# A z block computed around the last x_proj product, and gate tiles between the turnings at the switch of halves

## The reference, cut to what matters

```
xn = layernorm(x)                                  # x: (2, 1024, 512), everything in float32
xz = xn @ in_proj_w                                # 512 -> 2 * 1024: x and z
xc = silu(causal_conv4(x_part))
dt, B, C = rmsnorm each part of (xc @ x_proj_w.T)  # 32 + 16 + 16 columns
dt = softplus(dt @ dt_proj_w.T + dt_bias)
for each time step t, each of 16 states n, each of 1024 channels:
    h[n] = exp(dt * A[n]) * h[n] + dt * B[n] * xc
    y    = sum over n of C[n] * h[n]
s = ((y + D * xc) * silu(z)) @ out_proj_w.T
g = silu( down( silu(gate(xn)) * up(xn) ) )        # gate, up, down: dequantised weights and a low-rank part
out = x + s * g
```

## Time and profile before

| | |
|---|---|
| median of 3 runs | 1154.04 us (1153.87 to 1154.09) |
| profiled execution | 1153.82 us, of it span 1151.7 us |
| TensorE, VectorE, ScalarE, GpSimd busy | 96%, 80%, 59%, 64% of the span |
| mean granted clock of TensorE | 0.992 |
| chain that ended last | POOL 39%, PE 28%, issue 19%, DVE 11% |

### The profile page before, as it was taken

One profiled execution on the slowest core, in us unless ns is written; L12 is line 12 of the kernel. 1 busy time (PEld: TensorE's weight loads), 2 busy tenths in 40 slices (PEclk: granted clock), 3 DMA queues, 4 the chain that ended last, 5 costly groups with the idle time before them and its releaser, 6 DMA issues.

```text
span 1151.7 us, 12396 instructions
## 1 busy us (share of the span) xinstructions
PE 1103.5 (96%) x4366; PEld 589.5 (51%) x4366; DVE 926.9 (80%) x741; ACT 674.3 (59%) x850; POOL 734.7 (64%) x406
## 2 busy tenths in 40 slices
PE   5998999999999999999999899999999999999998
PEld 3443455555545555554443335555555455555543
DVE  4897999999789999996315469999987899999820
ACT  3224577877647777764022357777775477777410
POOL 2000799999537999980410048999983599999311
PEclk9998999999999999999999899999999999999999
DMA  7663289999914999999411124999984289998941
GB/s 248 218 205 128 100 206 235 249 243 225 247 54 118 241 238 261 209 201 315 174 37 36 46 82 130 239 238 250 240 205 149 84 207 247 242 238 193 280 181 43
DMA packets 62162, 215.44 MB, mean 187 GB/s; under 512 B 6762, under 2 KB 6890, under 8 KB 61588
## 3 DMA queue, kind: packets, MB, share of 16 engines
q0 software_dynamic: 16128, 88.09, 38.8%
q1 hardware_dynamic: 44388, 120.88, 30.9%
q10 hardware_dynamic: 1584, 5.68, 1.2%
HBM read 103.56 MB, written 22.98 MB: 110 GB/s over the span
## 4 chain that ended last, share of the span: by engine, by line
POOL 39%; PE 28%; issue 19%; DVE 11%; ACT 2%; DMA 1%; POOLq 0%; DVEq 0%; SPq 0%
POOL ub L627 34%; PE psM L1076 8%; PE psM L1015 6%; DVE hb L1253 5%; POOL yT L637 5%; PE psA L845 4%; PE psM L876 3%; PE psT L991 2%; DVE xc L1244 1%; DVE th L1103 1%; PE psA L961 1%; DMA yT<-yc 1%; DVE xc L1103 1%; DVE hid L1103 1%; PE psT L840 1%
## 5 line engine op out<-in xcount | busy, mean ns | idle before, releaser
L627 POOL TENSOR_TENSOR ub<-dtx,bn 128x1024 f32<-128x1024 f32 x256 | 647.0, 2590 | 275.0 <-DMA bn<-ss_rows_scratch 187.3
L1253 DVE TENSOR_TENSOR_SCAN hb<-psA,ub 128x1024 f32<-128x1024 f32 x256 | 581.7, 2280 | 26.4 <-POOL ub L627 23.2
L732 ACT ACTIVATE psA<-dt,cc 128x1024 f32<-128x1024 f32 x256 | 285.9, 1119 | 139.9 <-DVE hb L1253 138.0
L876 PE MATMUL psM<-xnT,w_ts 128*126 128x512 f32 x704 | 328.8, 598 | 3.5 <-DVE th L1103 3.5
L991 PEld LDWEIGHTS psT<-ident,hb 128*128 128x128 f32 x1984 | 226.9, 141 | 166.0 <-issue 82.5
L991 PE MATMUL psT<-ident,hb 128*128 128x128 f32 x1984 | 270.9, 275 | 13.1 <-DVE yT L1103 7.3
L753 ACT ACTIVATE yc<-psT,ssm 128x512 f32<-128x512 f32 x336 | 216.9, 679 | 20.9 <-PE psT L991 13.2
L876 PEld LDWEIGHTS psM<-xnT,w_ts 128*126 128x126 f32 x704 | 122.8, 190 | 114.8 <-issue 114.8
L1015 PE MATMUL psM<-w_dn,hid 126*128 126x512 f32 x352 | 163.3, 594 | 0.0
L1004 PE MATMUL psM<-xnT,w_ts 128*128 128x512 f32 x256 | 121.4, 593 | 0.0
L637 POOL DMA_DIRECT2D yT<-yc x112 | 111.2, 993 | 8.6 <-ACT yc L753 5.2
(11 more groups left out here) (85 smaller groups left out, 576.6 us busy)
## 6 DMA issues: line engine op xcount, KB each, us to landing
yT<-yc POOLq DMA_DIRECT2D x112, 768.0 KB, 8.4
bn<-ss_rows_scratch SPq DMA_DIRECT2D x66, 512.0 KB, 7.1
w_ts<-w_gu_scratch SPq DMA_DIRECT2D x44, 504.0 KB, 5.3
w_ts<-w_in_dram SPq DMA_DIRECT2D x32, 256.0 KB, 5.1
hb<-z_scratch SPq DMA_DIRECT2D x16, 512.0 KB, 7.3
z_scratch<-hid SPq DMA_DIRECT2D x28, 256.0 KB, 6.7
w_gu_scratch<-hid ACTq DMA_DIRECT2D x11, 504.0 KB, 5.1
yT<-x_dram SPq DMA_DIRECT2D x8, 512.0 KB, 8.9
```

The lines of the kernel that those rows point to most:

```text
L627: pool.tensor_tensor(ub[:, i % 2, :], dtx[:, i, :], bn[:, t, :], ALU.mult).then_inc(s_u, 1)
L732: act.activation(psA[:, i % 2, :], dt[:, i, :], ACT.Exp, scale=negA[:, h * DH + i, bass.ds(n, 1)]).then_inc(s_a, 1)
L876: mm = pe.matmul(psM[0:IM, gu, :], w_ts[:, off % 2, at:at + IM], xnT[:, k, h * CH:(h + 1) * CH], start=(k == 0), stop=(k == HK - 1))
L1253: dve.tensor_tensor_scan(hb[:, t * DH + i, :], psA[:, i % 2, :], ub[:, i % 2, :], 0.0, ALU.mult, ALU.add).then_inc(s_scan, 1)
```

## The change

Half 0's z block 0 leaves the tile list. Its weights are loaded during the in-projection into the free part of a weight slot; its first part is computed into `psA` ahead of the last `x_proj` product, one step behind it, three behind the transposing. ScalarE copies both parts in the tail. The gate step that stood there comes one transposing later. Half 0's list is now g0 to g3, g4, z1, g5, g6, z2, and so on, and all of its 44 down steps lie in the loop (before, the last 6 stood between the turnings at the switch). At the switch, gate tiles 0 and 1 of half 1 stand between the turnings. ScalarE's and VectorE's lists at the switch follow.

```diff
-TILES = [("g", n) for n in range(FILL + 1)] + [("z", 0), ("g", 4), ("g", 5), ("z", 1), ("g", 6), ...
+TILES = [[("g", 0), ("g", 1), ("g", 2), ("g", 3), ("g", 4), ("z", 1), ("g", 5), ("g", 6), ("z", 2), ...
...
-REST = 6
...
     if h == 0:
-        steps, at, n = STEPS[:-REST], p, QUARTERS
+        steps, at, n = STEPS[h], p, QUARTERS
...
+SP_ORDER = [[("z", 0, 0), ("z", 0, 1), ("G", 2), ("G", 3), ("G", 4), ("B", 2), ("Z", 1), ("B", 3), ...
...  SP
+                    if m + 2 == DB - 1:
+                        sp.dma_start(w_z0(b), w_in[DB]).then_inc(s_wz0, 16)
...
+                    if n == 1:
+                        sp.wait_ge(s_z0, 2 * b + 2)
+                    load_g(n, w_half(0, n), w_slot(b, w_half(0, n)))
...  ACT, tail
+                def copy_z0(c):
+
+                    t = TH_SLOTS["z", 0, c]
+                    act.wait_ge(s_z0, 2 * b + c + 1)
+                    act.wait_ge(s_ths[t], th_stored(b, 0, t, -1))
+                    act.activation(th_tiles[t], psA[:, 0, c * CH:(c + 1) * CH], ACT.Copy).then_inc(s_late, 1)
+
+                copy_z0(0)
                 act.wait_ge(s_xp, b + 1)
                 act.activation(xr, psM[:, 0, :], ACT.Copy).then_inc(s_xr, 1)
...
                 act.activation(rs[:, 0:1], mv[:, 0:1, 1], ACT.Softplus).then_inc(s_past, 1)
+                copy_z0(1)
...  ACT, switch
                         copy_late(h - 1, "d", JD - 1, 0)
-                        decay(0, 2)
                     for t in range(2):
                         act.wait_ge(s_ths[t], th_stored(b, h, t, -1))
                     ahead(0)
-                    if h == 0:
-                        decay(0, 2)
-                        ahead(1)
+                    decay(0, 2)
+                    ahead(1)
                     decay(0, 3)
...  PE, tail
+                for k in range(HK):
+                    z0_step(0, k)
                 x_proj(DB - 1).then_inc(s_xp, 1)
+                z0_step(1, 0)
...
                 mm.then_inc(s_xt, 1)
-                gate_up(b, 0, 0, 0)
+                for k in range(1, HK):
+                    z0_step(1, k)
...
                     mm.then_inc(s_tfa, 1)
+                gate_step(b, 0, 0, 0)
...  PE, switch
-                        for i in range(2):
+                        for i in range(DH):
                             turn_back(i)
-                            for kind, j, k in STEPS[len(STEPS) - REST + i * REST // 2:len(STEPS) - (1 - i) * REST // 2]:
-                                down(h - 1, j, k)
-                        for i in range(2, DH):
-                            turn_back(i)
-                            gate_up(b, h, 0, i - 2)
-                        for q in range(2, 4):
-                            gate_up(b, h, 0, q)
-                    for n in range(1, FILL):
+                            if i < 2:
+                                gate_up(b, h, 0, 2 * i)
+                                gate_up(b, h, 0, 2 * i + 1)
+                            else:
+                                gate_up(b, h, 1, 2 * i - 4)
+                                gate_up(b, h, 1, 2 * i - 3)
+                    for n in range(1 + h, FILL):
                         ahead(n)
...  DVE, switch
+                        drive(1, 3)
                         add_skip(0)
                         times_z(0)
-                        drive(1, 3)
                         add_skip(1)
                         scan(0, 0, 0)
+                        silu_gate(0, 0)
                         times_z(1)
                         add_skip(2)
+                        hidden(0, 0)
                         scan(0, 0, 1)
                         times_z(2)
                         add_skip(3)
-                        silu_gate(0, 0)
+                        silu_gate(1, 1)
                         scan(0, 0, 2)
-                        hidden(0, 0)
                         times_z(3)
+                        hidden(1, 1)
                         scan(0, 0, 3)
-                        silu_gate(1, 1)
-                        hidden(1, 1)
                         silu_gate(2, 0)
```

More of the change, by code:

```diff
@@ L217, in build, with w_slot, dt_views, w_z0 @@
         negA = cc[:, :, AL:AL + NS]
-        dt_slot = (DB + W_HALF + 1) % 2
-        ssT1 = [w_ts[c * R:(c + 1) * R, dt_slot, 0:CH] for c in range(HALVES)]
-        wdt1 = [w_ts[c * R:(c + 1) * R, dt_slot, CH:CH + DH * P] for c in range(HALVES)]
+        def w_slot(b, off):
+            return (b * W_USES + off) % 2
+        def dt_views(b, c):
+            t = w_slot(b, w_half(1, 1))
+            return w_ts[c * R:(c + 1) * R, t, 0:CH], w_ts[c * R:(c + 1) * R, t, CH:CH + DH * P]
+        def w_z0(b):
+            return w_ts[:, w_slot(b, DB - 1), CH:CH + HK * P].rearrange("p (k j) -> p k j", k=HK)
         psA = ctx.enter_context(nc.psum_tensor("psA", [P, 2, L], F32))
@@ L267, in build @@
         s_xc = sem("s_xc")
+        s_wz0 = sem("s_wz0")
+        s_z0 = sem("s_z0")
         s_wx = sem("s_wx")
@@ L356, in landed, with use @@
         def landed(b, off):
-            return b * (8 * W_USES) + 16 * (off // 2 + 1)
+            return 16 * (w_use(b, off) // 2 + 1)
         def w_half(h, n):
-            return DB + h * W_HALF + n
-        def use(kind, i):
-            return TILES.index((kind, i))
+            return DB + h * len(TILES[0]) + n
+        def use(h, kind, i):
+            return TILES[h].index((kind, i))
         def gated(b, h, n, gu):
@@ L538, in _ @@
                         load_b(1, 1)
-                    for what in SP_ORDER:
+                    for what in SP_ORDER[h]:
                         if what[0] == "B":
@@ L542, in _ @@
                         elif what[0] == "G":
-                            off = w_half(h, use("g", what[1]))
-                            load_g(what[1], off, off % 2)
+                            off = w_half(h, use(h, "g", what[1]))
+                            load_g(what[1], off, w_slot(b, off))
                         elif what[0] == "N":
@@ L820, in _ @@
                                 scale_y(n, tb)
-                    for what in ends(QUARTERS - 1, h):
-                        copy_late(h, *what)
+                    if h + 1 == HALVES:
+                        for what in ends(QUARTERS - 1, h):
+                            copy_late(h, *what)
                 for i in range(DH):
@@ L868, in gate_step @@
                 gu, k = divmod(step, HK)
-                off = w_half(h, use("g", n))
+                off = w_half(h, use(h, "g", n))
+                t = w_slot(b, off)
                 if step == 0:
-                    pe.wait_ge(s_w[off % 2], landed(b, off))
+                    pe.wait_ge(s_w[t], landed(b, off))
                 if k == 0 and (h or n):
@@ L922, in _, with z0_step @@
                         x_proj(m - 1)
+                def z0_step(c, k):
+                    if c == 0 and k == 0:
+                        pe.wait_ge(s_wz0, 16 * b + 16)
+                        pe.wait_ge(s_af, a_use(b, DB) + 1)
+                    mm = pe.matmul(psA[:, 0, c * CH:(c + 1) * CH], w_z0(b)[:, k, :], xnT[:, k, c * CH:(c + 1) * CH],
+                                   start=(k == 0), stop=(k == HK - 1))
+                    if k == HK - 1:
+                        mm.then_inc(s_z0, 1)
+                for k in range(HK):
+                    z0_step(0, k)
                 x_proj(DB - 1).then_inc(s_xp, 1)
+                z0_step(1, 0)
                 if b == 0:
```

92 lines of the change are left out of this document (52 added, 40 removed), and 7 rows, old and new, of the table SP_ORDER.

## The result

The changed kernel takes 1146.21 us (median of 4 runs, 1145.21 to 1146.77) against 1153.99 us before (4 runs, 1153.87 to 1154.09): a ratio of 0.9934, 95% interval 0.9922 to 0.9946, or 7.8 us less. The profiled execution took 1145.97 us with a span of 1143.9. The forecast was 1145.6. One of the twelve executions in experiment 3 ran at a mean granted clock of 0.559 and took 1930.76 us; it is left out there.

The account below looks back on a forecast made before the run. GpSimd was taken to bound mid-half, VectorE the switch, where TensorE's tiles came late. Tails -0.3 - 0.9, loops +0.6, B rows +0.4, switches -8.2 make -8.4 us: 1145.6 us, range 1143.5 to 1148.5, chance 0.57.

Parts of the forecast that it names:

- The switch: Change of halves, twice: gate tiles come earlier, VectorE's wait for tanh goes; -4.1 us each, -8.2 for two.
- the chain: VectorE's operations at the switch, timed singly: `add_skip` 322.96, `times_z(1)` until 330.01, next row's scan about 347.2, against 351.25.
- Rival 1: Switch: `times_z(1)` is not held by GpSimd's multiply; each switch gives 1.9 us more, 1141.8 us; chance 0.15.
- Rival 2: Switch: GpSimd comes first at `times_z(2)` and `times_z(3)` too, two more holds of 1.9 us, 1153.2; chance 0.12.
- The tail: Behind the in-projection: z steps fill TensorE's waits, the clock stays up; -0.3 us in batch 0, -0.9 in batch 1.
- rival 3: Tail: the clock still falls, each tail loses 1.6 us instead of gaining, 1150.0 us; chance 0.08.
- The B row: Z stores behind the first two B row loads, on which GpSimd's start hangs: +0.2 us per batch, bounds 0 and +3.4.
- Rival 4: First B row shares transfers with z stores and gate tile 1's load; at longest landing 6.6 us lost per batch, 1158.4; chance 0.08.
- The loop: First half's loop, 132 steps instead of 134: +0.3 us per batch, +0.6 for both, bounds 0 and 1.2.
- Gate tile 4: First half's loop: follows tile 3 at once, adding two VectorE operations of 0.61 us; later a z tile takes its place.
- What two matmuls more or less cost there is nothing: Middle of a half: GpSimd and VectorE pass rows round, TensorE fills what is left, so steps were priced at nothing.

Follow-up runs that it names:

- experiment 3: Changed kernel with the old order of the switch on TensorE, ScalarE and VectorE, still without down steps there: 1155.6 us, ratio 1.0006.
- experiment 4: Kernel before, with the new order of the switch on all three engines but its six down steps kept there: 1152.03 us, ratio 0.9981.
- experiment 2: Kernel before, with the switch part of the change alone (140 steps in the first half's loop, old tail): 1147.21 us, ratio 0.9941.
- experiment 1: Changed kernel with one exchange on VectorE at the switch, `silu_gate(0, 0)` behind `times_z(1)` instead of ahead: 1141.75 us, ratio 0.9889.
- Experiment 8: Kernel before, with four more unused matmuls ahead of the last `x_proj` in each batch: 1153.57 us over 12 runs, ratio 0.9995.
- experiment 7: Changed kernel with the two stores of z block 0 moved behind gate tile 3's load on SP's queue: 1144.61 us, ratio 0.9917.
- experiment 9: Changed kernel with the edits of experiments 1 and 7, and gate steps between the turnings parted 3, 5, 4, 4 instead of 4, 4, 4, 4: 1139.34 us.
- experiment 6: Changed kernel with the old switch (126 loop steps), row loads from the third on one place earlier on SP's queue: 1148.50 us, ratio 0.9950.
- experiment 10: Kernel of experiment 9 with each first-half row load one place earlier on SP's queue, 132 loop steps: 1138.09 us, ratio 0.9861.

## Why the prediction was right, and where its steps were not

**The switch,** forecast -4.1 each, measured -4.33 and -4.34. Each link of the chain came within 0.4 us of its forecast time: `add_skip(1)` at 322.83 (322.96), `times_z(1)` until 329.89 (330.01), the scan of row 1 at 346.84 (347.2). These times compare directly, since `add_skip(0)` starts within 0.1 us of where it was. Experiments 3 and 4 show that both the order and the absence of the down steps are needed for it, and experiment 2 that they give it without the tail.

**Rival 1** would have come true with `times_z(1)` ahead: it said 1.9 us per switch and 1141.8, and experiment 1, which makes it so, has 1.65 us and 1141.75; only 3.3 of the 4.5 us between the medians are the switches', so that closeness is partly luck. The Trainium skill's rule (SBUF — State Buffer, "Who interferes with whom": two SBUF inputs on VectorE against a GpSimd read, the first issued keeps the port) is shown here in both directions: 3.08 against 1.20 us, and 2.36 against 3.19. **Rival 2** did not happen: the other `times_z` took 1.19 to 1.23 us.

**The tail,** forecast -0.3 and -0.9, measured -0.59 and -1.18: the mechanism was right (**rival 3** is refuted: 1.00), the size 0.3 us too small in both. The gain came in three parts, by differences of starts in batch 0: up to `xr`'s copy 0.18 us (I had a loss of 0.06), over the transposing 0.41 (I had 0.45), and nothing was lost to the second z copy (I had 0.16). I had priced the copies by their durations of 0.60 us, but on ScalarE they follow each other by 0.48 and 0.54 us, and the first one began 0.1 us earlier than reckoned once the earlier start of this execution is taken off. Experiment 8 changes only the clock there and shortens batch 0's tail by 0.59 us too, though at another place: 0.56 up to `xr`'s copy, where here ScalarE's z copy takes the time.

**The B row** is the step that was mis-sized most. I put "0.2, near the lower end, because the second row's 512 KB were behind it before too"; it was 0.98 and 0.70, and experiment 7 shows that the z stores do it. **Rival 4** named this mechanism; the landing grew by 1.0 and 0.7 us, where 4.4 would have decided.

**The loop** was put at +0.3 per batch, with bounds of 0 and 1.2, and measured +0.26 and +1.23. Over the ten loops of 132 steps with this tail and the row loads' order of the change (after, experiments 1, 3, 7 and 9) it is 199.6 to 201.3, +0.9 in the mean: above my value, and at its longest outside my bounds. The list of steps is the same in all ten, so with a spread of 1.7 us the two values of the changed kernel alone say little. Gate tile 4 did what I reckoned: counted from multiply to multiply, the loop's fourth row in the changed kernel takes 11.4 us instead of 10.8, and the fifth 10.9 instead of 11.7. What is left over lies in later rows, single ones of some 12 us, at most 13.3, instead of 11. The longest two (13.0 and 13.3) contain waits of 0.94 and 1.30 us for a row load; batch 0 of experiment 3 has no such wait and takes 201.0, so they are not the whole of it.

The reason given for pricing two steps at nothing fails. "What two matmuls more or less cost there is nothing" and GpSimd as the only pace are contradicted where only the steps change, or little else: from 134 to 140 steps the loop is 1.2 us longer (experiment 2), and 126 steps give 196.9 and 197.1 us where 132 give 199.5 and 199.7, both with the rows early (experiments 6 and 10, which also differ in the z stores' place). I read a GpSimd share of 99% as the bound; but TensorE was at 98% in the same stretch. The count alone does not set the loop either, since 134 steps in the old list took 199.5 us. Whether TensorE's time or the place of the tiles among the quarters sets it stays open: no run here moves one without the other.

The sum was right to 0.6 us with errors that cancel: tails 0.6 and switches 0.5 us better than forecast, B rows 1.3 and loops 0.9 us worse, 0.7 us at the start that the change did not make, and 0.2 elsewhere. That the sum came so close is luck in part; the switch, its largest term, is not.

## What to carry to other kernels

When an engine waits, ask whose order holds its data back: taking work off TensorE gained nothing until VectorE read its tile earlier, and then the same work was in the way. Where GpSimd and VectorE multiply in the same stretch, place the short VectorE operation directly behind the scan that releases GpSimd, so that it starts first; here that was worth 1.65 us. Changing the number of steps in a loop also changes when its buffers come free; look at what stands behind those loads on the same queue before believing a time.

## What was not expected of the hardware

Two z stores of 256 KB issued right behind a row's load made that row, issued ahead of them, come 1.0 and 0.7 us later (3.9 against 4.9 us). And a pause that TensorE is spared can come back as another: with only the first gap filled, the granted clock of the profiled execution fell to 0.50 from 108 us on instead, and twelve executions of the same program took 1150.7 to 1159.0 us at mean clocks of 1.000 to 0.989.
